# A decoder layer with half-precision pairs for the second attention's weights and values, turned by DMA transposes, and a new order of work

## The reference, cut to what matters

```python
x = _layernorm(x + attn_1(x))       # 16 heads; logits against 64 latent keys, the best 4, softmax, latent values
x = _layernorm(x + attn_2(x, ctx))  # 16 heads; softmax over the batch's 64 context rows, then values, then Wo
x = _layernorm(x + ffn(x))          # three ternary weights; inputs rounded to 8 bits with a scale for each row

def attn_2(x, kv):                  # the part that the title speaks of
    ...
    scores = jnp.einsum('bhsr,bhlr->bhsl', q_r, k_r)
    attn = jax.nn.softmax(scores, axis=-1)
    ctx_c = jnp.einsum('bhsl,bld->bhsd', attn, kv_rope)
    ctx_lat = jnp.einsum('bhsd,hkd->bshk', ctx_c, w_kc_kv)
    return ctx_lat.reshape(b, s, H * K) @ Wo.T
def linear_bit(x, w, g):            # used three times in ffn
    xq = act_quant(rmsnorm(x, g))   # round(x * 127 / max|x|) * max|x| / 127
    return xq @ ternary_quant(w).T
```

## Time and profile before

| | |
|---|---|
| median of 3 runs | 366.12 us (365.68 to 366.55) |
| span of the profiled execution, first to last instruction | 364.8 us |
| what lies around the span (median less span) | 1.3 us |
| busy: PE, DVE, ACT, POOL | 335.7, 311.2, 261.4, 247.4 us |
| mean granted clock of TensorE | 0.985 |

### The profile page before, as it was taken

One profiled execution on the slowest core, in us unless ns is written; L12 is line 12 of the kernel. 1 busy time (PEld: TensorE's weight loads), 2 busy tenths in 40 slices (PEclk: granted clock), 3 DMA queues, 4 the chain that ended last, 5 costly groups with the idle time before them and its releaser, 6 DMA issues.

```text
span 364.8 us, 7459 instructions
## 1 busy us (share of the span) xinstructions
PE 335.7 (92%) x2549; PEld 249.6 (68%) x2549; DVE 311.2 (85%) x776; ACT 261.4 (72%) x467; POOL 247.4 (68%) x223
## 2 busy tenths in 40 slices
PE   8889998997799879999899989899999999998684
PEld 4587785785677557777677767677877778666342
DVE  2763467699979999989989999999999898998984
ACT  2536898972758549867889778578998588688762
POOL 3263725679976588794984959478879746768551
PEclk9969999999989999999999999999999999999999
DMA  7999920000000000000000000000000000000001
GB/s 214 237 364 362 368 109 2 0 3 1 2 0 2 1 3 0 2 0 17 6 11 16 1 1 2 16 15 3 2 14 3 14 16 0 16 16 14 5 27 44
DMA packets 6597, 17.58 MB, mean 48 GB/s; under 512 B 864, under 2 KB 3680, under 8 KB 5728
## 3 DMA queue, kind: packets, MB, share of 16 engines
...
## 4 chain that ended last, share of the span: by engine, by line
PE 43%; DVE 19%; POOL 18%; issue 12%; DMA 4%; ACT 2%; SPq 1%; POOLq 0%; DVEq 0%; ACTq 0%
PE wide L501 6%; PE small L539 6%; DMA region_c<-in_wkcqT 4%; PE wide L560 3%; PE wide L485 3%; PE wide L516 3%; POOL region_c L1344 3%; PE wide L434 3%; PE wide L422 2%; DVE m L997 2%; PE small L457 2%; POOL P L1320 2%; PE wide L334 2%; POOL Ls L1300 2%; PE wide L527 2%
## 5 line engine op out<-in xcount | busy, mean ns | idle before, releaser
L539 PE MATMUL small<-V_sb,PT_sb 128*128 128x256 f32 x256 | 58.7, 382 | 1.5 <-DVE y_row L1028 1.5
L539 PEld LDWEIGHTS small<-V_sb,PT_sb 128*128 128x128 f32 x256 | 47.6, 190 | 9.7 <-DVE y_row L1028 2.3
L1285 POOL TENSOR_TENSOR Ls<-Ls,m 128x1024 f32<-128x1024 f32 x16 | 31.4, 1961 | 28.2 <-DVE mask L1011 28.2
L501 PE MATMUL wide<-B_sb,x1T 128*128 128x512 f32 x192 | 49.6, 407 | 0.0
L1344 POOL TENSOR_TENSOR region_c<-region_c,region_q 128x1024 f32<-128x1024 f32 x16 | 33.2, 2072 | 16.4 <-DVE region_c L1135 13.6
L501 PEld LDWEIGHTS wide<-B_sb,x1T 128*128 128x128 f32 x192 | 35.5, 188 | 9.8 <-issue 1.4
L1292 POOL TENSOR_TENSOR mask<-mask,r 128x1024 f32<-128x1024 f32 x16 | 31.5, 1967 | 15.4 <-DVE r L1020 15.4
L1300 POOL TENSOR_TENSOR Ls<-Ls,mask 128x1024 f32<-128x1024 f32 x16 | 38.0, 2372 | 2.7 <-ACT Ls L753 2.0
L997 DVE MAX8 m<-Ls 128x8 f32<-128x64 f32 x256 | 33.9, 208 | 4.8 <-ACT Ls L740 4.7
L1320 POOL TENSOR_TENSOR P<-P,r 128x1024 f32<-128x1024 f32 x16 | 32.1, 2007 | 8.6 <-DVE r L1075 8.6
L560 PE MATMUL wide<-tern,region_k 128*128 128x512 bf16 x128 | 31.8, 379 | 0.9 <-ACT region_k L837 0.7
...
## 6 DMA issues: line engine op xcount, KB each, us to landing
xT<-in_xT SPq DMA_DIRECT2D x8, 256.0 KB, 8.8
...
region_t<-in_w2T SPq DMA_DIRECT2D x1, 1024.0 KB, 13.0
...
```

Of the source, the lines that this page charges most:

```text
L501: mm = pe.matmul(ps_L2[:, r * 512:(r + 1) * 512], x1T[:, u, k, :], B_sb[:, s, w, k, r * 512:(r + 1) * 512], start=(u == w == k == 0), stop ...
L539: mm = pe.matmul(ps_O2[:, 0:D], PT2_sb[:, c, :], V_sb[:, c, :], start=(c == 0), stop=(c == PAIRS - 1))
L1285: pool.tensor_tensor(heads(Ls[n % 2][:]), heads(Ls[n % 2][:]), over_heads(m8[:, :, 0:1]), ALU.subtract).then_inc(g_d1, 1)
```

## The change

Nearly every step is touched. What it does:

1. **Second softmax and values in half precision.** The weights `P2_sb` are divided by their sum scaled by 4096, copied to float16 (`high_P`, ScalarE), and the rest that float16 leaves is computed into a second float16 half (`low_P`, GpSimd). Both halves are turned by two DMA transposes of 128x1024 each from SP (`turn_high_P`, `turn_low_P`), in place of eight TensorE transposes and `copy_PT2`. The values are scaled by a factor from their squares (`square_C`, `square_kv`, `S4`, `value_scale`) and split the same way: `high_V` copies to float16, `VL` subtracts the copy in PSUM by a matmul with minus the identity, `low_V` copies the rest. `O2` is then 24 float16 matmuls of 256 columns (high by high, high by low, low by high).
2. **Logits of the second attention in float32.** `L2` is four float32 matmuls of 512 columns; `low_x1` and `low_B` are gone.
3. **Norms put off.** `norm_1` and `norm_2` are gone: the row before its norm is carried on, its root enters as the scale of `exp_2` and in `residual_2`, and the FFN's row scales take up the second root (`moments_2`, `roots_2`). `square_x2` and `roots_x` are gone. Weight 3 is centred (`centre_3`), so that the last norm is `square_3`, a root, and a scaled copy on ScalarE in place of VectorE's statistics and `norm_3`.
4. **First softmax.** The mask is bfloat16 and read from PSUM; `scale_mask` is gone; the division by the sum moves behind the values: `RT` turns the reciprocals (two TensorE transposes), `copy_R` copies them, `scale_AT` on VectorE takes the place of `copy_AT`. `gaps_4` moves to GpSimd.
5. **FFN inputs.** A packing step to float16 follows each rounding (`pack_x` of 512, `pack_h` of 1024 columns, ScalarE). For tiles 0 to 11 DMA transposes (`turn_x`, `turn_h`) take the place of `XQT`, `HT` and their copies; tiles 12 to 15 keep TensorE's.
6. **Buffers, loads, order.** PSUM is four areas of 1024 columns, given out by a table for each step and tile; most working tiles exist twice; the loads are fewer and larger, with the context behind the first weights; and the order of all engines is new.

```diff
+            def turn_x(n):
+                sp.wait_ge(a_px, n + 1)
+                since(sp, p_Z2, n - 1)
+                sp.dma_start_transpose(xqT[n % 2], xq16[n % 2]).then_inc(t_x[n % 2], 16)
+            def turn_high_P(n):
+                sp.wait_ge(a_P16, n + 1)
+                since(sp, p_O2, n - 1)
+                sp.dma_start_transpose(PT16[n % 2][:, 0:PAIRS], P16[n % 2][:, 0:WIDE]).then_inc(t_P[n % 2], 16)
+            def turn_low_P(n):
+                sp.wait_ge(g_lo2, n + 1)
+                sp.dma_start_transpose(PT16[n % 2][:, PAIRS:2 * PAIRS], P16[n % 2][:, WIDE:2 * WIDE]
+                                       ).then_inc(t_PL[n % 2], 16)
...
+            turn_high_P(0); turn_high_P(1); turn_low_P(0); turn_low_P(1); turn_x(0); turn_high_P(2)
+            turn_low_P(2); turn_x(1); turn_high_P(3); turn_low_P(3); turn_high_P(4); turn_low_P(4)
...
             def L2(n, *freed):
...
-                for u, w in PARTS:
-                    if u == 1:
-                        pe.wait_ge(v_xlo, n + 1)
-                    for k in range(KD):
-                        for r in range(2):
-                            mm = pe.matmul(ps_L2[:, r * 512:(r + 1) * 512], x1T[:, u, k, :],
...
+                for k in range(KD):
+                    for r in range(2):
+                        mm = pe.matmul(pair(HOME_L2, n)[:, r * 512:(r + 1) * 512], x1T[n % 2][:, k, :],
+                                       B_sb[:, n // 2 % 2, k, r * 512:(r + 1) * 512],
+                                       start=(k == 0), stop=(k == KD - 1))
...
+            def VL(half, b):
...
+                for r in range(2):
+                    c = r * 4 + 2 * half
+                    mm = pe.matmul(pair(HOME_V, 2 * b + half)[:, r * 512:(r + 1) * 512].rearrange(
+                                       "p (c d) -> p c d", c=2), minus_ident16[:], V16[:, b % 2, 0, c:c + 2, :],
+                                   start=False, stop=True, skip_group_check=True)
...
             def O2(n, *freed):
...
-                for c in range(PAIRS):
-                    mm = pe.matmul(ps_O2[:, 0:D], PT2_sb[:, c, :], V_sb[:, c, :],
-                                   start=(c == 0), stop=(c == PAIRS - 1))
+                pe.wait_ge(t_P[n % 2], 16 * (n // 2 + 1))
+                for u, w in PARTS:
+                    if u == 1:
+                        pe.wait_ge(t_PL[n % 2], 16 * (n // 2 + 1))
+                    for c in range(PAIRS):
+                        mm = pe.matmul(bank(HOME_O2, n)[:, 0:D], PT16[n % 2][:, u * PAIRS + c, :],
+                                       V16[:, b % 2, w, c, :], start=(u == w == c == 0),
...
+            def high_P(n):
+                act.wait_ge(g_P2, n + 1)
+                since(act, t_P[n % 2], 16 * (n // 2))
+                since(act, t_PL[n % 2], 16 * (n // 2))
+                act.activation(P16[n % 2][:, 0:WIDE], P2_sb[n % 2][:], ACT.Copy).then_inc(a_P16, 1)
...
+            def pack_h(n):
...
+                act.activation(hq16[n % 2], hg[n % 2], ACT.Copy, bias=-ROUND).then_inc(a_ph, 1)
...
+            def scale_AT(n):
...
+                dve.tensor_tensor(AT[n % 2][:], bank(HOME_WT, n)[:, 0:D].rearrange("p (k t) -> p k t", k=KD),
+                                  R_sb[n % 2][:], ALU.mult).then_inc(v_AT, 1)
...
+            def low_P(n):
+                pool.wait_ge(a_P16, n + 1)
+                pool.wait_ge(g_P2, n + 1)
+                pool.tensor_tensor(P16[n % 2][:, WIDE:2 * WIDE], P2_sb[n % 2][:], P16[n % 2][:, 0:WIDE], ALU.subtract
+                                   ).then_inc(g_lo2, 1)
```

More of the change, by code:

```diff
@@ new lines, in _ @@
+            low_V(0, 2); copy_B(1, 1); copy_PT1(7); copy_R(7); copy_L1(9); copy_B(2, 1); whole_x(0)
+            copy_X1(4); exp_2(3); high_P(2); pack_x(0); copy_B(3, 1); square_1(4); exp_4(9); whole_x(1)
+            copy_L1(10); copy_PT1(8); square_1(5); exp_1(9); pack_x(1); high_P(3); tanh(0); square_1(6)
+            copy_X1(5); exp_2(4); square_2(2); square_h(0); tanh(1); high_V(1, 2); low_V(1, 2); high_P(4)
+            copy_R(8); exp_2(5); square_2(3); copy_PT1(9); high_V(0, 3); copy_X1(6); copy_L1(11)
@@ new lines, in _ @@
+            copy_R(9); whole_x(2); pack_x(2); low_V(0, 3); high_P(5); copy_X1(7); whole_h(0); exp_1(10)
+            exp_4(10); exp_2(6); square_1(7); copy_Q(6); pack_h(0); square_1(8); exp_1(11); tanh(2)
+            copy_B(0, 2); whole_x(3); square_h(1); copy_B(1, 2); copy_PT1(10); copy_X1(8); pack_x(3)
+            exp_2(7); square_2(4); copy_B(2, 2); square_2(5); copy_L1(12); copy_PT1(11); tanh(3)
+            copy_B(3, 2); high_P(6); high_P(7); square_3(0); exp_4(11); high_V(1, 3); copy_R(10)
@@ new lines, in _ @@
+            whole_h(1); pack_h(1); copy_L1(13); copy_Q(7); exp_4(12); norm_3(0); low_V(1, 3); whole_x(4)
+            pack_x(4); exp_1(12); square_h(2); exp_2(8); copy_X1(9); high_V(0, 4); copy_R(11); tanh(4)
+            square_1(9); whole_h(2); square_3(1); pack_h(2); square_h(3); exp_4(13); low_V(0, 4)
+            high_P(8); copy_PT1(12); exp_2(9); norm_3(1); square_2(6); whole_x(5); pack_x(5); copy_X1(10)
+            square_3(2); square_1(10); high_V(1, 4); copy_R(12); whole_h(3); exp_1(13); square_h(4)
@@ new lines, in _ @@
+            square_2(7); square_1(11); low_V(1, 4); copy_X1(11); copy_R(13); copy_L1(14); high_V(0, 5)
+            norm_3(2); high_P(9); whole_x(6); pack_h(3); pack_x(6); low_V(0, 5); tanh(5); exp_2(10)
+            whole_h(4); pack_h(4); copy_PT1(13); exp_1(14); high_P(10); copy_L1(15); square_h(5)
+            exp_4(14); exp_2(11); square_1(12); tanh(6); square_3(3); copy_B(0, 3); copy_B(1, 3)
+            square_2(8); copy_B(2, 3); high_V(1, 5); whole_x(7); copy_B(3, 3); pack_x(7); exp_4(15)
@@ new lines, in _ @@
+            low_V(1, 5); square_h(6); whole_x(8); copy_R(14); square_3(4); copy_X1(12); norm_3(3)
+            copy_PT1(14); tanh(7); pack_x(8); whole_h(5); pack_h(5); square_2(9); high_P(11); square_h(7)
+            tanh(8); square_1(13); exp_1(15); norm_3(4); whole_h(6); pack_h(6); copy_X1(13); square_3(5)
+            square_2(10); high_V(0, 6); exp_2(12); whole_x(9); pack_x(9); high_V(1, 6); square_h(8)
+            low_V(0, 6); low_V(1, 6); whole_h(7); high_P(12); tanh(9); copy_X1(14); square_1(14)
@@ new lines, in _ @@
+            norm_3(5); exp_2(13); square_3(6); pack_h(7); square_h(9); copy_PT1(15); whole_h(8)
+            pack_h(8); whole_x(10); pack_x(10); square_2(11); copy_R(15); whole_h(9); high_P(13)
+            pack_h(9); norm_3(6); exp_2(14); high_V(0, 7); tanh(10); square_3(7); whole_x(11)
+            square_1(15); square_2(12); copy_X1(15); square_3(8); high_P(14); norm_3(7); square_h(10)
+            low_V(0, 7); pack_x(11); whole_x(12); pack_x(12); high_V(1, 7); norm_3(8); exp_2(15)
+            low_V(1, 7); copy_XQ(12); square_2(13); tanh(11); whole_h(10); high_P(15); tanh(12)
@@ L923, in _ @@
+            pack_h(14); square_h(15); square_3(13); norm_3(12); copy_HT(14); whole_h(15); pack_h(15)
+            norm_3(13); square_3(14); copy_HT(15); norm_3(14); square_3(15); norm_3(15)
         @block.vector
@@ L1040, in low_x1 @@
[L1040 to L1053 removed]
+                dve.tensor_tensor(y1[n % Y1_HOMES], bank(HOME_O1, n)[:, 0:D], bo_row[:], ALU.add
+                                  ).then_inc(v_y1, 1)
@@ L1218, in _ @@
-            low_B(0, 3); moments_3(5); low_B(1, 3); largest_x(8); scale_x(8); low_B(2, 3)
-            low_x1(12); low_B(3, 3); residual_1(13); max_8(15); gaps_4(15); norm_2(9); norm_3(5)
-            gate_2(7); residual_3(6); top_4(15); largest_x(9); norm_1(13); scale_x(9); sum_2(11)
-            residual_1(14); sum_4(15); largest_h(7); scale_h(7); max_2(12); shift_2(12)
-            gate_1(8); residual_2(10); low_x1(13); gate_2(8); sum_2(12); norm_1(14)
-            moments_3(6); gate_1(9); norm_3(6); norm_2(10); max_2(13); residual_3(7)
```

1228 lines of the change are left out of this document (622 added, 606 removed).

## The result

The changed kernel takes 357.34 us, median of four runs (355.07 to 358.26), beside 365.90 us for the kernel before on the same chip (365.19 to 366.55): a ratio of 0.976, 95% interval 0.972 to 0.980. The forecast was 344. The direction was right, the gain of 8.6 us was well under half of the 22 foreseen. The profiled execution of the changed kernel has a span of 353.3 us, 11.5 less than the 364.8 before; it is the fastest of the four (355.07 us). Ratios are formed without the executions that ran in a slower state (one of e6's four, 359.14 us, which is also its profiled one, and one of e8's, 355.54), while medians have all.

A forecast was written before the change was run, and what follows sets the result against it. PE and DVE, each 94% busy in the loop, were taken to bound the kernel as a pair. Span 364.8 - 20 - 2 + 2 + 1 = 345.8, less 3 is 342.8, with 1.3 around it 344 us; range 322 to 376.

The forecast's parts named there:

- The bound before: Loop of the kernel before: PE and DVE, each 94% busy, bound it as a pair; relieving one alone gains little.
- the 14.5 us that PE stood for DVE: Nine entries of PE waiting for DVE, placed in the loop; part of this would go, -3 us net.
- PE: TensorE's busy time over the whole span: its terms sum to -18.3 us, to 317.
- Net about -46, to 265: DVE's busy time over the span: groups of 71.7 us go, new steps come, leaving 265 us.
- small ones: New small DVE steps, a 256-wide reciprocal, centre_3 and a longer residual_2: some 9 us in all.
- 13.0: DVE: four new steps a tile (scaled sum, moments_2, third scale, moments_3), priced as one-column steps at 0.203 us.
- -3: DVE: two scale steps become one, 3 us less.
- if DVE stays above 290, a term of mine was missed: Sign against the forecast: DVE busy above 290 us, where about 265 was foreseen, means a missed term.
- 33 us more: ACT's net rise in busy time, to 295 us; in the loop from 201.7 to 235, beside PE's 235.5.
- -20 - 3 + 2 = -21: Loop: 20 us less at 94% fullness, 3 less PE standing for DVE, 2 more for transfers in SP's list.
- -2 + 1: Ends: head 2 us shorter by earlier loads; tail 1 us longer by pack_h and the last softmax's transfers.
- Rival 1: PE stands less: all 14.5 us of waits for DVE go and L2 is cheapest, 325 us; chance 0.08.

The follow-up runs named there:

- e6: Changed kernel with the 256-column reciprocal made over 16 sums and spread by two copies on GpSimd: 357.25 us, ratio 0.969.
- e8: e6 with the rounding of h to whole numbers also left out: 351.65 us, ratio 0.955.
- e7: Kernel before with only second attention's scores (L2) in float32 and low_x1, low_B gone: 370.84 us, ratio 1.009.
- e2: Changed kernel with the 256-column reciprocal on DVE done twice: 385.76 us, ratio 1.050.
- e15: Changed kernel with the largest of h taken over 64 of 1024 columns (scale of h wrong): 355.38 us, ratio 0.971.
- e13: Changed kernel, same mathematics: narrow reciprocal spread by reductions, second sums' scaling and moments' sum on GpSimd, two-column scale step split: 348.27 us, ratio 0.952.
- e14: e13 with the rounding of h to whole numbers left out: 342.95 us, ratio 0.937.

## Why the prediction was wrong, point by point

**The bound before**: right as far as it was tried. Relief of DVE alone gains nothing, as e7 shows (DVE -20.5, time +0.9%); relief of PE alone was not tried there. Of the 14.5 us that PE stood for DVE, 12.0 lie between 75 and 345 us; the forecast had all nine entries in the loop.

**PE**: right in sum, 319.8 for 317; O2 was 5.2 us shorter than foreseen, VL 2.1 and RT (6.4 for 4.2) 2.2 longer. Luck has a part in the sum: PE's groups overlap (they add up to 367.9 us before and 345.9 after, where PE was busy 335.7 and 319.8), so differences of groups don't simply add up to that of the engine.

**DVE**: the step that failed, and it was a term of the sum that was mis-sized. "Net about -46, to 265" was -14. The 256-wide reciprocal cost 28.0 us where its share of the "small ones" was 16 x 0.410 = 6.6: 21.4 us. The new few-column steps had 10 us net in the forecast, "13.0" for four steps priced by a one-column row and "-3" for two steps that become one. They measured 26.4: 6.7 for the one of sixteen columns, 8.5 for the one of three, 6.3 for the two of one column, and 10.2 for the two-column step that took the place of two (5.3). That is 16.4 us over, and 13.4 of it stand over the groups' own medians, as waits for GpSimd. Together 37.8 us, more than the 32.2 by which DVE was over; the rest went the other way in terms that the sum left out, first the narrow reciprocal that the wide one replaced (4.0). The kernel before showed the wait too, in norm_2, 354 ns in the middle and 2376 at most:

```profile
L1091 DVE TENSOR_SCALAR region_q<-y_row,root x16: 345/354/2376, 92.3 to 339.1; 128x256 f32<-128x256 f32 x16
```

So DVE did not stop "being part of the bound" as forecast: it was busy for 95% of the loop, and e2's added work on it was paid in full. Yet e6 and e15, with 18 and 14 us off it, gained little, so its load was not all that set the time. e13 put the term right, at the forecast's 265 us, and got 9 of the missing 13 us. The prediction's own sign, "if DVE stays above 290, a term of mine was missed", was met.

**ACT**: right in size, wrong in place. The forecast put all of its 33 us more into the loop and had PE and ACT "both about 94%" there. In the cut above ACT has 200.71 of 232.5 us in the loop, 86%, and in the tail 45.90 of 51.4 where it had 32.81 of 48.5; late stages take pack_h, norm_3 and square_3 of the last tiles at once. PE stood 4.4 us more in the tail than before: its waits for ACT there rose from 5.2 to 7.7 us, those for DVE from 1.9 to 3.5. The two longest, at the transposes `HT` of the last tiles and at `O3`:

```profile
PE wide L651 <- ACT w_raw L966: 2.8, 3, 1.2
PE wide L665 <- ACT w_raw L972: 2.3, 3, 1.1
```

The lower granted clock of this tail (0.93 of full speed on average, 1.00 before) explains little of its length: e13's tail, at 0.99, still took 50.20 us. e14, with 14 us off ACT (and h not rounded), brought the rest of the gain: a span of 316.55 us of PE's work and 24.6 of standing, beside the 317 + 25.8 of the forecast.

**The loop itself** went from 253.6 to 232.5 us, -21.1, where the prediction had -20 - 3 + 2 = -21. That this came out is partly luck: the forecast's loop was the stretch from 75 to 345 us, not this cut, and 5.4 us of PE work had moved into the head, so the loop also had less to do.

**Ends**: -2 + 1 was forecast, +6.7 and +2.9 came. The larger part of the head's growth is work moved ahead of the first max_2; in e13 the head is 2.1 us shorter. So "relief in the loop plus small ends" was the wrong form of sum: a new order moves work across the border of the stages, and only the whole counts.

**Transfers**: right that they are hidden, 3.2 us for 2.6, and the 2 us put down for them were not needed. **Rival 1** (PE stands less) went the other way, by 4.3 us.

**The range** of 322 to 376 held the time.
